# Row sums of the second attention layer between the shared expert products, and the last stage's weight preparation moved to the scores

## The reference

```
h = h + _L0_ffn_ref(_layernorm(h), ...)     # shared expert for all tokens + one of 8 routed experts per token
h = h + _L1_attn_ref(_layernorm(h), ...)    # 8-bit integer attention
h = h + _L1_ffn_ref(_layernorm(h), ...)     # three blocks of 4-bit weights with low-rank corrections

# in _L0_ffn_ref
shared_out = _swiglu(x, shared_gate, shared_up, shared_down)
return (shared_out + routed_out).reshape(b, s, h)
# in _L1_attn_ref
xq, xs = quant_act(query, 8)                # one scale: max |x| over all tokens
q, _ = quant_linear(xq, xs, wq, bq)         # b_s = w_s * x_scale, b_int = round(b / b_s)
aw = jnp.einsum('ntd,nsd->nts', q, k)       # the scores, again quantised by one scale
# in _L1_ffn_ref
w = (q / 7.5 - 1.0) * jnp.repeat(scale, GROUP, axis=1)
```

## Time and profile before

| | before |
|---|---|
| median of 3 runs | 574.7 us (573.93 to 576.48) |
| profiled execution | 579.41 us |
| its span, first to last instruction | 577.6 us |
| PE busy | 419.8 us (73%) |
| DVE busy | 324.2 us (56%) |
| ACT busy | 246.2 us (43%) |
| POOL busy | 143.9 us (25%) |
| mean granted TensorE clock | 0.832 |

### The profile page before, as it was taken

The page is one execution under the profiler, slowest core; times in us unless marked ns, Lnnn a source line. Parts: engine busy times, 40 slices in busy tenths (PEclk is TensorE's granted clock), DMA queues, the critical chain, the costliest instruction groups (busy, mean ns, idle before and its releaser), DMA issues.

```text
span 577.6 us, 8904 instructions
## 1 busy us (share of the span) xinstructions
PE 419.8 (73%) x3189; PEld 306.6 (53%) x3189; DVE 324.2 (56%) x876; ACT 246.2 (43%) x512; POOL 143.9 (25%) x169
## 2 busy tenths in 40 slices
PE   3677884477779979999889993362497114699997
PEld 3545652256568965666555782221243013489996
DVE  3858875489653410232411116868898995645642
ACT  4235444256634411222212211396099476286661
POOL 3544433089721150000000053800000000213410
PEclk9969887569997997999999998685555555599999
DMA  8921111293003332111101071000000000000002
GB/s 278 406 99 17 20 17 14 82 425 167 2 1 146 111 109 83 36 56 37 49 25 43 23 291 37 0 1 3 1 1 0 1 2 2 1 1 0 1 19 68
DMA packets 19789, 38.59 MB, mean 67 GB/s; under 512 B 2136, under 2 KB 16164, under 8 KB 18340
## 3 DMA queue, kind: packets, MB, share of 16 engines
q1 hardware_dynamic: 18788, 35.41, 17.7%
q0 software_dynamic: 960, 2.62, 1.3%
HBM read 29.77 MB, written 7.01 MB: 64 GB/s over the span
## 4 chain that ended last, share of the span: by engine, by line
PE 46%; DVE 28%; issue 11%; ACT 8%; POOL 5%; DMA 2%; SPq 1%; DVEq 0%; ACTq 0%
PE psum L1253 11%; PE psum L1285 5%; PE psum L2334 4%; PE psum L2367 3%; PE psum L1260 3%; POOL ring L782 2%; PE psum L1299 2%; PE psum L610 2%; PE psum L2373 2%; ACT experts L1662 1%; POOL experts L787 1%; PE psum L921 1%; PE psum L1277 1%; DMA experts<-in_tern 1%; PE psum L2351 1%
## 5 line engine op out<-in xcount | busy, mean ns | idle before, releaser
L1253 PE MATMUL psum<-experts,ring 128*128 x136 | 67.1, 619 | 1.6 <-issue 1.2
L1084 DVE TENSOR_TENSOR ring<-ring,psum 128x512 f32<-128x512 f32 x17 | 11.7, 688 | 67.9 <-PE psum L1253 67.9
L1184 POOL DMA_INDIRECT front<-expert_results,slot_of x10 | 9.5, 953 | 126.4 <-DMA expert_results<-ring 123.7
L1260 PE MATMUL psum<-front,shared 128*128 128x256 f32 (+1 forms) x160 | 36.8, 383 | 0.0
L1253 PEld LDWEIGHTS psum<-experts,ring 128*128 128x128 f32 x136 | 24.4, 199 | 21.0 <-issue 20.9
L1260 PEld LDWEIGHTS psum<-front,shared 128*128 128x128 f32 x160 | 30.3, 197 | 3.5
L1285 PE MATMUL psum<-experts,ring 128*128 x136 | 32.1, 379 | 0.0
L1285 PEld LDWEIGHTS psum<-experts,ring 128*128 128x128 f32 x136 | 25.8, 190 | 10.3 <-issue 7.7
L1382 ACT COPY ring<-psum 128x512 f32<-128x512 f32 x17 | 10.0, 586 | 42.3 <-PE psum L1277 42.3
L2334 PE MATMUL psum<-experts 128*128 128x256 f32 (+1 forms) x120 | 27.4, 371 | 0.0
L590 PE MATMUL psum<-experts,ring 128*128 128x256 f32 x108 | 26.1, 393 | 0.8 <-DVE experts L485 0.7
(11 more groups left out here) (361 smaller groups left out, 1085.7 us busy)
## 6 DMA issues: line engine op xcount, KB each, us to landing
experts<-in_experts SPq DMA_DIRECT2D x8, 1536.0 KB, 12.5
experts<-in_x SPq DMA_DIRECT2D x9, 384.0 KB, 8.3
expert_rows<-zeros SPq DMA_DIRECT2D x1, 2176.0 KB, 14.8
ring<-expert_rows SPq DMA_DIRECT2D x17, 128.0 KB, 2.2
shared<-in_shared SPq DMA_DIRECT2D x1, 1536.0 KB, 18.0
experts<-in_ffn_q SPq DMA_DIRECT2D x1, 1536.0 KB
experts<-in_ffn_s SPq DMA_DIRECT2D x1, 1536.0 KB
experts<-in_pos_embed SPq DMA_DIRECT2D x1, 1152.0 KB, 9.6
```

The lines of the kernel that those rows point to most:

```text
L1084: nc.vector.tensor_tensor(o, o, up_bank(g), ALU.mult).then_inc(hidden_done.sem, 1)
L1253: mm = nc.tensor.matmul(bank, sl_xT[t % 2][:, k, :], slot_w(t, block, k, F), start=(k == 0), stop=(k == KD - 1))
L1260: mm = nc.tensor.matmul(o[:, b, 0:w], shared_w(block, k, (2 * half + b) * P, P), moe_x(c)[:, k, 0:w], start=(k == 0), stop=(k == KD - 1))
```

## The change

Two things move; no arithmetic is added or left out, and one wait is added.

- The row sums of chunks 0 and 1 go into `moe_vector`, between shared_added(3) and hidden(26). Those of chunks 2 and 3, and the shifts of chunks 0 and 1, go between hidden(26) and shared_added(4). What is left in `l1_rows_vector` is the sum of chunk 4, three shifts and five peaks. The shifts of chunks 2 and 3 now stand ahead of the first peak.
- `lora_pool` waits, besides its loads, for `l1_s_ready.done(0)`: the copy of the first tile of scores.

```diff
@@ moe_vector, the loop over groups g
                     nc.vector.tensor_copy(sl_y[t % 2], psum[:, 2, 0:D]).then_inc(sl_y_ready.sem, 1)
+                if g == GROUPS:
+                    row_sums(dve, step, 2)
+                    row_sums(dve, step, 3)
+                    row_shift(dve, 0)
+                    row_shift(dve, 1)
                 if g >= 1 and shared_step(g - 1) is not None and shared_step(g - 1)[1] == 1:
                     shared_added(shared_step(g - 1)[0])
+                if g == GROUPS - 2:
+                    row_sums(dve, step, 0)
+                    row_sums(dve, step, 1)
@@ l1_rows_vector (row_sums is the old summed, row_shift the body of the old centred)
-            for c in range(NT // 2):
-                summed(c)
-                if c >= 2:
-                    centred(c - 2)
-                if c >= 3:
-                    peaked(c - 3)
+            row_sums(dve, step, 4)
+            centred(2)
             centred(3)
+            peaked(0)
+            peaked(1)
+            centred(4)
             peaked(2)
-            centred(4)
             peaked(3)
             peaked(4)
@@ lora_pool
             pool.wait_ge(l_ffn.sem, l_ffn.all)
+            pool.wait_ge(l1_s_ready.sem, l1_s_ready.done(0))
```

More of the change, by code:

```diff
@@ L1545, in tower, with row_sums @@
         x_s, q_s, aw_s, x0, bq_i, cq_i = (small[:, i:i + 1] for i in range(6))
+        def row_sums(dve, step, c):
+            dve.wait_ge(rows_back[c], 32)
+            dve.wait_ge(sh_added.sem, sh_added.done(c))
+            nc.vector.tensor_tensor(h[:, 2 * c:2 * c + 2, :], h[:, 2 * c:2 * c + 2, :], moved[:, 2 * c:2 * c + 2, :], ALU.add).then_inc(step.sem, step.one())
+            dve.wait_ge(step.sem, step.sofar())
+            for t in (2 * c, 2 * c + 1):
+                nc.vector.bn_stats(hst6[:, t, :], h[:, t, :]).then_inc(step.sem, step.one())
+            dve.wait_ge(step.sem, step.sofar())
+            nc.vector.memset(gate[:, :], 0.0)
+            for t in (2 * c, 2 * c + 1):
+                nc.vector.bn_aggr(hst[:, t, :], hst6[:, t, :]).then_inc(step.sem, step.one())
+            dve.wait_ge(step.sem, step.sofar())
+            nc.vector.tensor_scalar(var_eps[:, 2 * c:2 * c + 2], hst[:, 2 * c:2 * c + 2, 1], LN_EPS, None, ALU.add).then_inc(row_var.sem, 1)
@@ L1547, in l1_rows_vector, with row_shift @@
+        def row_shift(dve, c):
+            dve.wait_ge(row_rstd.sem, row_rstd.done(c))
+            nc.vector.scalar_tensor_tensor(neg_mr[:, 2 * c:2 * c + 2], hst[:, 2 * c:2 * c + 2, 0], -1.0, rstd[:, 2 * c:2 * c + 2],
+                                           ALU.mult, ALU.mult).then_inc(row_ready.sem, 1)
         def l1_rows_vector(dve, step):
             nc.vector.memset(round_b[:, :], ROUND)
[L1550 to L1562, removed]
@@ L1564, in centred @@
             def centred(c):
-                dve.wait_ge(row_rstd.sem, row_rstd.done(c))
-                nc.vector.scalar_tensor_tensor(neg_mr[:, 2 * c:2 * c + 2], hst[:, 2 * c:2 * c + 2, 0], -1.0, rstd[:, 2 * c:2 * c + 2],
-                                               ALU.mult, ALU.mult).then_inc(row_ready.sem, 1)
+                row_shift(dve, c)
             def peaked(c):
```

## The result

| | before | changed |
|---|---|---|
| median, runs side by side | 575.4 us (4 runs, 573.93 to 576.48) | 568.74 us (4 runs, 566.53 to 570.81) |
| ratio, with 95% interval | | 0.9882 (0.9855 to 0.991) |
| profiled execution | 579.41 us, span 577.6 | 570.12 us, span 568.3 |

The ratio means 5.2 to 8.3 us less. The forecast was 563.4 us with a range of 560.0 to 567.0; the median lies above it. The direction was right, the size was not. The two profiled executions differ by 9.3 us, more than the medians do; the experiments show that 2.1 us of it come from a gap that a second trace of the old kernel doesn't have.

What follows compares the result with a forecast made beforehand. It took the row sums, last in DVE's list, and DVE and GpSimd blocking each other behind the peak as the bounds: 7.0 + 4.6 - 0.3 = 11.3 us off 574.7 gives 563.4 us, range 560.0 to 567.0.

Steps and rivals of the forecast that it cites:

- this stall costs nothing either way: At L1089, 2.2 us behind PE's up product in the old trace: the two early sums would fill that gap.
- part one: Row sums moved earlier into DVE's idle time: last peak 7.0 us sooner, bounds 5.0 to 8.0.
- Steps 1 and 2: Two sums ahead of L1089 run from 344.5 to 348.3, so L1089 starts 0.85 us later, bounds 0 to 2.5.
- The rule on two inputs in SBUF: Early sums' adds could wait for GpSimd's gather instructions, 0.95 us each, 1.9 together; nothing taken, since these only write descriptors.
- rival (a): Early sums held up by GpSimd's gathers (1.9 us) or late landings (1.4): total 565.3 to 566.7 us, chance 0.17.
- Step 3: Behind L1089 two sums and two shifts nearly hide behind PE's last down product; last add ends at 353.7.
- The paragraph on TensorE's clock: Clock in the projections or ahead of the last stage may differ: about 1 us either way, range widened by 1.5.
- Step 4: From the last add, the fifth sum, shifts and peaks follow; last peak ends at 359.7 instead of 366.73.
- Part two: GpSimd's twelve instructions moved from behind the peak into the scores: projections start at 372.6, not 377.19, gain 4.6 us.
- The cast: Among the scores, L1645 meets GpSimd's first conversion and waits 0 to 0.6 us; 0.3 taken as lost.
- (c): L1089 so late that the sums' gain is lost at the down product: 570.4 us, chance 0.01.
- (d): Slower than before because the last stage loses the high clock: 578.4 us with 15 us lost, chance 0.03.

Runs made afterwards that it cites:

- r4: Changed kernel with the two 1536 KB loads for the last stage issued only after the last gather has landed: 566.55 us, ratio 0.9836.
- r6: Changed kernel with 14 unneeded products added on PE behind the last up product: 569.05 us, ratio 0.988.
- r9: Changed kernel with 7 unneeded products added on PE behind the last up product: 568.43 us, ratio 0.9857.
- r2: Kernel before with only the row sums and shifts moved, without the added wait in lora_pool: 570.66 us, ratio 0.9915.
- r5: Changed kernel run once more, nothing altered, for a second trace and more times: 567.97 us, ratio 0.9879.
- r1: Kernel before run once more, nothing altered, for a second trace: 574.99 us in a single execution.
- r3: Kernel before with only the added wait in lora_pool, row sums where they were: 570.38 us, ratio 0.9913.
- r7: Changed kernel with L1089 ahead of all row sums, those of chunks 0 and 1 before the last add, the others behind it: 567.61 us, ratio 0.9858.
- r10: Changed kernel with loads after the last gather, chunk 0's sum before shared_added(3), GpSimd's preparation waiting for the second scores tile: 564.58 us, ratio 0.9791.

## Why the prediction was wrong

**What bounds the kernel: half right.** That the sums stood last in DVE's list, and that GpSimd held up the small operations, both stood the test. But I read one trace as the kernel. Its 2.2 us without work ahead of L1089 had no cause in any row, and the prediction said so; it then reasoned that "this stall costs nothing either way", since the early sums would fill it. That is true of the changed kernel only. The kernel before without the gap is 2.1 us faster to the peak, and the gain about that much smaller. The same trace was 4.7 us over the median, and I wrote that "the steps named are short operations that should not differ between them". One of them did. The sum should have taken the gap as present or absent, with 0 to 2.2 us off part one. This was the first step that failed.

**Steps 1 and 2, the sums ahead of L1089: times right, price wrong.** First sum and L1089 came within 0.2 us of the forecast on the old clock. Against the old trace without the gap L1089 is 3.3 us behind the up product instead of 0.1, so the two sums cost 3.2 us where the step had 0.85. That is the same gap once more, not a further loss. The rule on two inputs in SBUF took nothing: L1559 takes 0.68 to 0.69 us beside the gathers. There GpSimd was the one that gave way: a gather that started at 344.34, 0.2 us behind the first L1559, took 1.31 us instead of 0.95. In r4 one that started 0.05 us behind such an add took 1.46. It agrees with the Trainium skill, page "SBUF — State Buffer", section "Who interferes with whom", in that whoever starts first keeps the port. The same section's inference that issuing a descriptor doesn't need the read side, for which the prediction took nothing, doesn't agree with these gathers; and on who loses, rival (a) was wrong.

**Step 3, the last down product: a term left out.** It was taken over at 3.87 us. It takes 5.50, since PE's longer wait lets the clock fall (r6 and r9). This was the second step that failed. The paragraph on TensorE's clock looked at the projections and the last stage, not at the place where the change itself lengthens PE's wait: 1.6 us.

**Step 4, the rest: right.** From the last add to the last peak the changed trace takes 6.7 us (354.09 to 360.79); forecast 6.9 (352.8 to 359.7).

With both set right, part one gives 7.0 - 2.2 - 1.6 = 3.2 us; r2's trace shows 3.1, the changed kernel's 3.2 (28.5 to 25.25).

**Part two: right.** 4.6 forecast; from the last peak's end to the projections the repeated old trace takes 10.8 us (362.56 to 373.39), the changed one 6.4 (360.79 to 367.21): 4.4. The cast cost 0.4 for a forecast of 0.3, the reduces kept their 0.68 us, and GpSimd was done 6.6 us early.

**The sum.** 3.2 + 4.4 - 0.4 = 7.2 us, against 6.7 and 7.6 by the two pairs of medians. So of the 5.3 us by which the forecast of 563.4 was missed, 4.1 are the sum's (11.3 to 7.2), 0.7 the median of the kernel before, which a fourth run moved from 574.7 to 575.4, and 0.5 are within what repeated runs differ by.

**The rivals.** None of the five was the one that came as a whole. (a) is nearest, with L1089 late, but by another mechanism; (c) named the right place, what the sums win being lost at the down product, and asked for a delay of 7 us; the price beyond the 0.85 taken was 2.3 us of delay and 1.6 of clock, and took half of part one. (d) had the slow start of the last stage, which did come in one of the two traces of the changed kernel, at 1.2 us. The range ended at a gain of 7.7 us (574.7 - 567.0); the gap of 2.2 us was in no bound, and with it the range would have held the 6.7.

## What to carry to other kernels

Work moved into an engine's idle time has to fit behind the instruction that others wait for, or be done before that instruction could run: measure its price from the moment at which that instruction could have run, and look at what the longer wait does to the waiting engine's clock. A gap in one trace that no row explains is to be taken as present or absent in the sum, above all when that execution lies above the median. And a transfer whose data is wanted late should not be issued beside one that is wanted now: here a single wait on SyncE was worth 3.1 us to the peak, as much as all of part one, half of it through PE's clock.

## What the runs showed of the hardware

- PE's last down product takes 5.50 us, most of it at the lower clock, after a wait of 3.85 to 4.00 us (r2, r5 and the changed kernel), and 3.86 to 3.87 us at the higher after 0.7 to 2.9 us (the old trace, r1, r3, r4, r7 to r10). In r6 and r9 work that nobody needs kept the clock up.
- The last stage, from its first product to the end, took 75.0 to 75.2 us in three traces (the changed kernel's first, r4, r6) and 73.9 to 74.4 in the nine others; in the first of the three the clock was at its lower level for the first 2.9 us.
- An indirect gather of 128 rows of 1 KB landed 2.6 to 7.3 us after its issue (median 4.2) beside two loads of 1536 KB, and 2.7 to 3.1 us (median 2.8, r4) without them.
- A gather's instruction that started 0.2 us behind a DVE add with two inputs in SBUF took 1.31 us instead of 0.95 (changed kernel); one that started 0.05 us behind took 1.46 (r4).
- A signal from PE reached DVE late twice in one execution of the kernel before: at 347 us by 2.1 us, with neither engine busy, and at 214 us by 1.5, where nothing on the chain waited for it. None of the eleven other traces has a wait that the rows call "remote" at L1089.
- The first 330 us, alike in all kernels, took 331.7 to 336.1 us up to the first gather. That is the size of the spread between executions of one kernel.
